# An attention and SwiGLU block on one core: the context reaches the output projection by DMA instead of by two rounds of transposes

## The chip, the cores and the metric

The kernel runs on one core of a Trainium2 chip. The metric is the device time of one execution in microseconds (us), lower is better. Before the change it was run three times: 753.49, 754.30 and 754.54 us, median 754.3 us. One more execution was profiled.

## The reference

Input `x` is (4, 1024, 128): batches, tokens, channels. With a LayerNorm `xn` of `x`, the output is `x + attention(xn) + ffn(xn)`.

```
q = xn Wq' + bq -> 16 heads of 8;  k, v = xn Wk' + bk, xn Wv' + bv -> 4 heads of 8, each shared by 4 query heads
q, k = rope(q), rope(k)
probs   = softmax(q k' / sqrt(8)) over 1024 keys
context = probs v                     # (4, 1024, 128)
attention = context Wo' + bo
ffn = (silu(xn Wg') * (xn Wu')) Wd'   # hidden 384, weights are int32 times 1/127
```

## The kernel before, in words

The attention is cut in 16 **groups**, one for each batch and key head: group `g` is batch `g // 4`, key head `g % 4`, and holds four query heads. A group runs 16 **steps**: two halves (`h`) of 512 queries by eight tiles of 128 keys. In each step:

- TensorE makes four score tiles of 128 keys x 512 queries (`scores`, line 1143) into three PSUM banks that are used in turn, and weighs the values by the probabilities of the step before (`weigh`, line 1229), all four heads into one PSUM bank, `acc_ps`, 32 rows a head: 8 rows of context, a row with the sum of the probabilities, the rest zero.
- ScalarE takes the exponential of each score tile (line 719).
- VectorE finds the row maxima for later halves from four more score tiles (`max_unit` line 1123 on TensorE, `reduce_max` line 946 on VectorE), which pass through a ring of four PSUM banks.

Beside the four maxima a step may hold a **job** that takes a slot of the same ring: the feed-forward part (`GATE`, `UP`, `DOWN`), the transposing of the negative maxima (`NEG_T`), and the context's way to the output. The table `JOB_AT` gives each step's jobs, and all engines issue in program order by it. `NEG_T` stands at steps 5 and 13: ScalarE copies its result, SyncE sends it by DMA (`load_neg`, line 434) into the rows of `qc` that the scores of the next half read two steps later.

The context's way before: when a half ends, ScalarE copies `acc_ps` to `acc_sb` (line 820). The job `CTX` at steps 8 and 16 transposes the four 128x128 tiles (line 1244) so that queries lie on partitions, and VectorE inverts the sums (line 979) and multiplies (line 981) into `ctx_all`. When the four groups of a batch are through, the job `STAGE` at step 9 transposes them back (line 1252), ScalarE copies the result to `ctx_T` (line 711; the tile is `v_T` under another name, and the profile calls it that), and `PROJ` at steps 12 and 14 multiplies by `Wo` (line 1279); VectorE adds that to `y_all` (line 998). Batch 0 is put out in groups 5 and 6, batch 1 in 9 and 10, batch 2 in 13 and 14, the first half of batch 3 in group 15. The last half of group 15 is done behind the last step (`CTX_END`, `STAGE_END`), because nothing is left to hide it.

SyncE issues the loads: at a group's start the parts for the next group's scores, after `NEG_T` of step 5 those for the maxima two groups on (`load_parts`, lines 408 to 423), each behind waits in one fixed order (`group` under `@block.sync`), and at the end the 16 stores of the output (line 506).

## Time and profile before

| | |
|---|---|
| median of three runs | 754.3 us (753.49 to 754.54) |
| profiled execution, its own time | 752.47 us |
| its span | 750.3 us |
| TensorE matmul busy | 718.9 us, 96% |
| VectorE busy | 682.7 us, 91% |
| ScalarE busy | 624.2 us, 83% |
| GpSimd busy | 227.0 us, 30% |
| DMA, mean | 51 GB/s |

The span is measured from the first to the last event of the profile; the execution's own time has 2.2 us more around it. A step is read best from the starts of `weigh` (line 1229): from one to the next is one step of all engines. A group takes 43.0 us, one that also puts out a half batch 43.4 us, and the groups fill the time from 60 us on. In these rows PE is TensorE, DVE VectorE, ACT ScalarE, POOL GpSimd, SPq the issuing of DMAs by SyncE.

### The profile page before, as it was taken

What the parts mean: (1) busy time and instruction counts of PE and PEld (TensorE: products, weight loads), DVE (VectorE), ACT (ScalarE), POOL (GpSimd) and SP (SyncE); (2) the same over time, 40 slices, a digit from 0 to 9 for tenths busy, and PEclk for the clock granted to TensorE, in tenths of its full rate; (3) what the DMA queues carried; (4) which work ended last, traced back from release to release, by engine and by line L of the source; (5) the groups of instructions that cost most, each with busy time, mean ns of one, the idle gap of its engine ahead of it and who ended that gap; (6) DMA issues with size and microseconds to landing.
All of it is one profiled execution on the core that took longest, in us unless ns stands there. A gap on an engine that the chain in (4) does not pass through costs nothing.

```text
span 750.3 us, 13756 instructions
## 1 busy us (share of the span) xinstructions
PE 718.9 (96%) x4914; PEld 216.2 (29%) x4914; DVE 682.7 (91%) x1265; ACT 624.2 (83%) x1305; POOL 227.0 (30%) x372
## 2 busy tenths in 40 slices
PE   7899999999999999999999999999999999999987
PEld 6332222222322222222322222232322222232222
DVE  6899999999999999999999999999999999999931
ACT  5638989888888988888888888889788888989886
POOL 3776552256331662112111212211121211202100
PEclk9999999999999999999999999999999999999999
DMA  9524331110311131010111101011111101110030
GB/s 298 176 65 110 117 118 33 33 34 2 117 34 33 33 115 35 5 43 19 33 33 33 33 24 43 2 34 33 33 33 33 33 2 33 33 33 2 2 85 29
DMA packets 30723, 38.26 MB, mean 51 GB/s; under 512 B 5600, under 2 KB 20448, under 8 KB 30400
## 3 DMA queue, kind: packets, MB, share of 16 engines
q1 hardware_dynamic: 27680, 30.18, 14.1%
q0 software_dynamic: 1440, 4.72, 1.7%
q10 hardware_dynamic: 1536, 2.49, 1.0%
q8 instruction: 39, 0.64, 0.4%
q14 instruction: 28, 0.23, 0.1%
HBM read 23.28 MB, written 11.53 MB: 46 GB/s over the span
## 4 chain that ended last, share of the span: by engine, by line
PE 75%; DVE 16%; ACT 6%; issue 2%; DMA 1%; SPq 0%; ACTq 0%; DVEq 0%
PE acc_ps L1229 29%; PE banks L1123 20%; DVE mx L946 13%; PE banks L1143 10%; PE banks L1096 7%; ACT probs L719 5%; PE banks L1236 4%; PE banks L1244 3%; PE banks L1063 1%; PE banks L1069 1%; DMA y_all<-in_x 1%; PE banks L1279 1%; PE banks L1252 1%; DVE stats L853 1%; DVE row_max L952 0%
## 5 line engine op out<-in xcount | busy, mean ns | idle before, releaser
L946 DVE TENSOR_REDUCE mx<-banks 128x1 f32<-128x512 f32 x1024 | 637.6, 682 | 27.1 <-PE banks L1123 24.0
L719 ACT ACTIVATE probs<-banks 128x512 f32<-128x512 f32 x1024 | 549.1, 606 | 91.3 <-PE banks L1143 86.1
L1143 PE MATMUL banks<-qc,kc 51*128 51x512 bf16 x1024 | 304.8, 382 | 10.6 <-ACT probs L719 5.5
L1123 PE MATMUL banks<-ka,qa 48*128 48x512 bf16 x1024 | 302.0, 382 | 7.1 <-DVE mx L946 6.9
L1229 PE MATMUL acc_ps<-probs,v_grp 128*32 128x512 f32 x2048 | 272.7, 605 | 1.2 <-ACT probs L719 1.0
L1123 PEld LDWEIGHTS banks<-ka,qa 48*128 48x128 bf16 x1024 | 67.2, 94 | 292.0 <-DVE mx L946 247.6
L577 POOL TENSOR_TENSOR neg_max<-row_max,nought 128x16 bf16<-128x16 f32 x32 | 7.1, 222 | 315.5 <-DVE row_max L952 310.2
L1143 PEld LDWEIGHTS banks<-qc,kc 51*128 51x128 bf16 x1024 | 64.5, 94 | 44.2 <-ACT probs L719 40.9
L1096 PE MATMUL banks<-xn_T,w_ffn 128*128 128x256 f32 x188 | 65.8, 434 | 0.0
L1229 PEld LDWEIGHTS acc_ps<-probs,v_grp 128*32 128x32 f32 x2048 | 40.3, 108 | 85.5 <-ACT probs L719 59.1
L601 POOL TENSOR_TENSOR gated<-gu 128x256 f32<-128x256 f32 x48 | 35.2, 734 | 73.7 <-ACT gu L808 73.7
L1096 PEld LDWEIGHTS banks<-xn_T,w_ffn 128*128 128x128 f32 x188 | 28.5, 189 | 38.7 <-DVE mx L946 25.1
L604 POOL TENSOR_TENSOR th<-th,gated 128x256 f32<-128x256 f32 x48 | 34.9, 726 | 3.8
L606 POOL TENSOR_TENSOR hid<-th,gated 128x256 f32<-128x256 f32 x48 | 34.9, 726 | 3.8
L1236 PE MATMUL banks<-w_ffn,hid 128*128 128x128 f32 x192 | 29.9, 292 | 0.0
L1236 PEld LDWEIGHTS banks<-w_ffn,hid 128*128 128x128 f32 x192 | 23.8, 190 | 13.7 <-DVE mx L946 6.9
L593 POOL COPY v_grp<-v_all 128x64 f32<-128x64 f32 x16 | 3.8, 239 | 70.1 <-PE acc_ps L1229 69.3
L1244 PE MATMUL banks<-ident,acc_sb 128*128 128x128 f32 x124 | 19.4, 279 | 2.8 <-ACT acc_sb L820 1.3
L820 ACT ACTIVATE acc_sb<-acc_ps 128x512 f32<-128x512 f32 x31 | 18.6, 598 | 0.5
L998 DVE TENSOR_TENSOR y_all<-y_all,banks 128x256 f32<-128x256 f32 x16 | 6.6, 412 | 12.8 <-PE banks L1279 12.8
L805 ACT ACTIVATE gu<-banks 128x256 f32<-128x256 f32 x45 | 18.1, 402 | 0.0
L1244 PEld LDWEIGHTS banks<-ident,acc_sb 128*128 128x128 f32 x124 | 13.0, 141 | 17.1 <-issue 9.3
(110 smaller groups left out, 349.3 us busy)
## 6 DMA issues: line engine op xcount, KB each, us to landing
qa<-q_rows SPq DMA_DIRECT2D x28, 192.0 KB, 3.5
qc<-q_rows SPq DMA_DIRECT2D x56, 96.0 KB, 2.6
q_rows<-part POOLq DMA_DIRECT2D x18, 256.0 KB, 4.2
ka<-k_later SPq DMA_DIRECT2D x24, 96.0 KB, 2.2
kc<-k_later SPq DMA_DIRECT2D x24, 96.0 KB, 2.2
out<-y_all SPq DMA_DIRECT2D x16, 128.0 KB, 2.0
y_all<-in_x SPq DMA_DIRECT2D x3, 512.0 KB, 12.3
k_rows<-part SPq DMA_DIRECT2D x6, 256.0 KB, 3.0
```

Of the source, the lines that this page charges most:

```text
L601: nc.gpsimd.tensor_tensor(gated[:, c, :], gu[:, c, 0:CH], gu[:, c, CH:2 * CH], ALU.mult).then_inc(gated_done, 1)
L604: nc.gpsimd.tensor_tensor(th[:, c, :], th[:, c, :], gated[:, c, :], ALU.mult).then_inc(gated_done, 1)
L606: nc.gpsimd.tensor_tensor(hid[:, c, :], th[:, c, :], gated[:, c, :], ALU.add).then_inc(hid_done, 1)
L719: nc.scalar.activation(probs[:, s % SLOTS, j, :], banks[:, score_bank(g, G * s + j), :], ACT.Exp, scale=SCALE).then_inc(exp_done, 1)
L820: nc.scalar.activation(acc_sb[:, s // NT, :], acc_ps[:, :], ACT.Copy).then_inc(acc_copied, 1)
L946: nc.vector.tensor_reduce(out=mx[:, h, col, k:k + 1], in_=ps, op=ALU.max, axis=AX.X).then_inc(max_done, 1)
L1096: nc.tensor.matmul(ps, w_ffn[:, n * HID + c * P:n * HID + (c + 1) * P], xn_T[:, chunk * CH:(chunk + 1) * CH], start=True, stop=True).then_ ...
L1123: nc.tensor.matmul(ps, qa[par][rows, j // 2, t * P:(t + 1) * P], ka[par][rows, k * W:(k + 1) * W], start=True, stop=True).then_inc(a_ready, 1)
L1143: nc.tensor.matmul(banks[:, score_bank(g, u), :], kc[par][rows, kt * P:(kt + 1) * P], qc[par][rows, h, j // 2, :], start=True, stop=True). ...
L1229: last = nc.tensor.matmul(acc_ps[VC * j:VC * (j + 1), :], v_grp[par][:, kt, :], probs[:, s % SLOTS, j, :], start=(kt == 0), stop=(kt == NT ...
L1236: last = nc.tensor.matmul(ps[:, 0:D], hid[:, c, t * P:(t + 1) * P], w_ffn[:, 2 * HID + c * D:2 * HID + (c + 1) * D], start=(c == 0), stop= ...
L1244: last = nc.tensor.transpose(ps[:, t * P:(t + 1) * P], acc_sb[:, h, t * P:(t + 1) * P], ident[:, :])
```

## The change

`CTX` and `STAGE` leave the table of jobs. SyncE moves each head's eight context rows from `acc_sb` straight to the rows of `ctx_T` that the projection reads (`move_context`): four DMAs of 8 x 512 a half. Beside each goes a DMA for the sums: for batches 0 to 2 one row of 512 to DRAM (`sums_rows`), and for batch 3 eight rows (there are eight columns of ones beside the values now) to `last_sums`. Once a batch the sums come back as 128 x 128, VectorE inverts them (`invert`), they go to DRAM again, and come back spread over eight partitions a head (`load_inverse`); VectorE multiplies `ctx_T` by them, 128 x 512 a half (`divide`). For batch 3 VectorE inverts `last_sums` itself, 128 x 512 in the last group. ScalarE's copy of `acc_ps` now waits until the half's last moves have landed. Twelve of the sixteen stores are issued ahead of the last group's moves. The end after the last step keeps its two transposes, of which the second is a matmul on the 32 rows that are new.

```diff
-JOB_AT = {..., 7: (UP, 1), 8: (CTX, 0), 10: (GATE, 2), 11: (UP, 2), 13: (NEG_T, 0), 16: (CTX, 1)}
+JOB_AT = {..., 7: (UP, 1), 10: (GATE, 2), 11: (UP, 2), 13: (NEG_T, 0)}
 def output_steps(u):
-    return {9: (STAGE, u), 12: (PROJ, 2 * u), 14: (PROJ, 2 * u + 1)}
+    return {12: (PROJ, 2 * u), 14: (PROJ, 2 * u + 1)}
 # SyncE
+            def move_context(g, h):
+                b = g // KV
+                sp.wait_ge(acc_copied, NH * g + h + 2)
+                if b > 1 and g % KV == 0:
+                    sp.wait_ge(o_ps, 2 * NH * (b - 1))
+                for j in range(G):
+                    ...
+                    sp.dma_start(ctx_T[rows, b % 2, h, :], acc_sb[VC * j:VC * j + HD, h, :]).then_inc(moved[h], 16)
+                    if b < B - 1:
+                        sp.dma_start(sums_rows[b:b + 1, n:n + W], acc_sb[VC * j + HD:VC * j + HD + 1, h, :]).then_inc(moved[h], 16)
+                    else:
+                        sp.dma_start(last_sums[rows, h, :], acc_sb[VC * j + HD:VC * j + 2 * HD, h, :]).then_inc(moved[h], 16)
             def group(g, par, left):
                 if left > 1:
                     sp.wait_ge(pv_done, STEPS * g + SLOTS)
                     load_parts(g + 1, qc[1 - par], kc[1 - par], qc_loaded[1 - par])
+                if g > 0:
+                    move_context(g - 1, 1)
                 load_neg(g, 1, par)
+                if g % KV == 0 and g > 0:
+                    load_sums(g // KV - 1)
+                if g % KV == 1 and g > KV:
+                    load_inverse(g // KV - 1)
+                if left == 1:
+                    store_out(0, 2 * OUTS - 4)
+                move_context(g, 0)
                 if g == 0:
                     ...                      # stores of the later parts, as before
                     load_parts(g + 2, qa[par], ka[par], qa_loaded[par])
+                if g % KV == 0 and g > 0:
+                    store_inverse(g // KV - 1)
                 if left > 1:
                     load_neg(g + 1, 0, 1 - par)
 # ScalarE
                         act.wait_ge(pv_done, STEPS * g + s + 1 + SLOTS)
+                        if g > 0:
+                            act.wait_ge(moved[s // NT], MOVES * g)
 # VectorE
+            def divide(u):
+                b, h = u // 2, u % 2
+                if b < B - 1:
+                    dve.wait_ge(spread_in[h], 16 * (b + 1))
+                    by = spread
+                else:
+                    dve.wait_ge(moved[h], MOVES * NG)
+                    nc.vector.reciprocal(last_sums[:, h, :], last_sums[:, h, :]).then_inc(last_inverted, 1)
+                    dve.wait_ge(last_inverted, 2)
+                    by = last_sums
+                nc.vector.tensor_tensor(ctx_T[:, b % 2, h, :], ctx_T[:, b % 2, h, :], by[:, h, :], ALU.mult).then_inc(divided, 1)
 ...
+                elif kind == GATE and n == FC - 1:
+                    if g % KV == 0 and g > 0:
+                        invert(g // KV - 1)
+                    if g in OUT_AT:
+                        divide(OUT_AT[g][12][1] // 2)
+                elif kind == NEG_T and g == NG - 1:
+                    divide_rest()
+                    divide(OUTS - 2)
 # TensorE
             def project_out(u, ps):
                 if u < 2 * OUTS - 2:
-                    pe.wait_ge(ctx_T_done, u // 2 + 1)
+                    pe.wait_ge(divided, u // 2 + 1)
```

How the instructions move, on TensorE first: around step 8 of a group, where line 1123 is a maximum's tile, 1143 a score tile, 1244 the transposes. Before:

```order
L1123 MATMUL banks<-ka,qa 128x512
L1143 MATMUL banks<-qc,kc 128x512
L1244 MATMUL banks<-ident,acc_sb 128x128 x4
L1123 MATMUL banks<-ka,qa 128x512
L1143 MATMUL banks<-qc,kc 128x512
L1229 MATMUL acc_ps<-probs,v_grp 32x512 x4
```

The same place now, the line numbers being those of the changed file:

```order
L1196 MATMUL banks<-ka,qa 128x512
L1216 MATMUL banks<-qc,kc 128x512
L1196 MATMUL banks<-ka,qa 128x512
L1216 MATMUL banks<-qc,kc 128x512
L1302 MATMUL acc_ps<-probs,v_grp 32x512 x4
```

Only the four transposes are gone between the third and the fourth pair.

SyncE's queue in the last group, before: the last negative maxima, then the stores.

```order
L434 DMA qc<-neg_max_T 3x8x128 [waits neg_T_done]
L434 DMA qc<-neg_max_T 3x8x128
L506 DMA out<-y_all 128x2x128 [waits o_done] x16
```

Now, the first of the four pairs of moves shown once:

```order
L441 DMA qc<-neg_max_T 3x8x128 [waits neg_T_done]
L441 DMA qc<-neg_max_T 3x8x128
L490 DMA out<-y_all 128x2x128 [waits o_done] x12
L502 DMA ctx_T<-acc_sb 8x512 [waits acc_copied]
L507 DMA last_sums<-acc_sb 8x512
```

Eight moves stand behind twelve stores; four stores follow them.

VectorE in the last group, behind the last row maxima, before:

```order
L952 TENSOR_TENSOR row_max<-mx 128x16 [waits max_done,neg_step]
L979 RECIPROCAL rec<-banks 128x16 [waits ctx_ps]
L981 TENSOR_TENSOR ctx_all<-banks,rec 128x4x32 [waits rec_done]
L998 TENSOR_TENSOR y_all<-y_all,banks 128x256 [waits o_ps] x2
```

Now:

```order
L1001 TENSOR_TENSOR row_max<-mx 128x16 [waits max_done,neg_step]
L1046 RECIPROCAL last_sums<-last_sums 96x512 [waits moved1]
L1048 TENSOR_TENSOR ctx_T<-ctx_T,last_sums 96x512 [waits last_inverted]
L1036 RECIPROCAL last_sums<-last_sums 128x512 [waits moved0]
L1039 TENSOR_TENSOR ctx_T<-ctx_T,last_sums 128x512 [waits last_inverted]
L1064 TENSOR_TENSOR y_all<-y_all,banks 128x256 [waits o_ps] x2
```

Two wide reciprocals and two wide products stand where a reciprocal of 16 columns and one product stood, and the second pair waits for the last group's moves.

## Rows read from the trace of the kernel before

**Rows 1.** The page: busy time of each engine, and the ending chain by engine.
```profile
PE 718.9 (96%) x4914; PEld 216.2 (29%) x4914; DVE 682.7 (91%) x1265; ACT 624.2 (83%) x1305; POOL 227.0 (30%) x372
PE 75%; DVE 16%; ACT 6%; issue 2%; DMA 1%; SPq 0%; ACTq 0%; DVEq 0%
```

**Rows 2.** Critical chain, group 7, steps 15 and 16: start us, duration us, what.
```profile
400.41 0.99 PE acc_ps L1229 x8
...
401.85 0.61 ACT probs L719
...
402.89 0.99 PE acc_ps L1229 x8
...
404.69 0.63 PE banks L1244 x4
...
405.64 0.99 PE acc_ps L1229 x8
```

**Rows 3.** Timeline of ACT there: start, us, engine, line, operation.
```profile
403.95 0.60 ACT L820 ACTIVATE acc_sb<-acc_ps 128x512 f32<-128x512 f32 x1
404.45 2.06 ACT L719 ACTIVATE probs<-banks 128x512 f32<-128x512 f32 x4
```

**Rows 4.** Critical chain, step 8 of group 7.
```profile
381.81 1.00 PE acc_ps L1229 x8
...
384.57 0.99 PE acc_ps L1229 x8
```

**Rows 5.** Critical chain, step 9 of group 6, which holds STAGE.
```profile
341.13 0.99 PE acc_ps L1229 x8
...
343.80 0.99 PE acc_ps L1229 x8
```

**Rows 6.** Timeline of DVE, group 6, first maxima of step 12.
```profile
347.85 2.48 DVE L946 TENSOR_REDUCE mx<-banks 128x1 f32<-128x512 f32 x4 [0.22 <-PE banks L1123]
```

**Rows 7.** By source line: DVE durations, ns min/median/max.
```profile
L915 DVE TENSOR_TENSOR ctx_all<-ctx_all,part x2: 689/864/1039, 16.9 to 21.0; 128x512 f32<-128x512 f32 x2
L979 DVE RECIPROCAL rec<-banks x31: 245/247/258, 83.0 to 728.5; 128x16 f32<-128x16 f32 x31
L989 DVE RECIPROCAL rec<-banks x2: 197/202/208, 744.7 to 745.1; 128x8 f32<-128x8 f32 x2
```

**Rows 8.** Timelines of ACT, SP and PE in group 0, in this order.
```profile
80.92 0.60 ACT L820 ACTIVATE acc_sb<-acc_ps 128x512 f32<-128x512 f32 x1
...
75.15 1.59 SPq L434 DMA_DIRECT2D qc<-neg_max_T  x2
...
86.60 0.90 SPq L420 DMA_DIRECT2D qa<-q_rows  x2
...
96.17 1.53 SPq L434 DMA_DIRECT2D qc<-neg_max_T  x2
...
99.38 0.60 PE L1143 MATMUL banks<-qc,kc 51*128 51x512 bf16 x2
```

**Rows 9.** Timeline of SP in group 15.
```profile
721.91 1.44 SPq L434 DMA_DIRECT2D qc<-neg_max_T  x2
723.40 6.37 SPq L506 DMA_DIRECT2D out<-y_all  x12
```

**Rows 10.** By source line: moves between places in SBUF, issue ns, then landing.
```profile
L459 SPq DMA_DIRECT2D xn<-xn x8: 586/589/686, 54.6 to 59.2; - x8
...
DMA to landing us min/median/max: 2.3/2.6/3.1
```

**Rows 11.** Timeline of PE, group 15: PROJ of step 12, and the last weigh.
```profile
736.06 0.71 PE L1279 MATMUL banks<-wf_sb,v_T 128*128 128x128 f32 x4
...
742.58 1.07 PE L1229 MATMUL acc_ps<-probs,v_grp 128*32 128x512 f32 x8 [0.57 <-ACT probs L719]
```

**Rows 12.** Windows early on: us, busy us (instructions) by engine, PEclk, DMA.
```profile
5.00:9.00 4.00, 4.00 (x21) 4.00 (x20) 2.83 (x19) 1.93 (x6) 0.00 (x0) 1.00 1.17 317
10.00:12.00 2.00, 1.87 (x17) 1.63 (x16) 2.00 (x9) 1.80 (x10) 0.00 (x0) 1.00 1.00 374
```

More of the change, by code:

```diff
@@ L78 @@
 NEG_BEHIND = HU + 5
-MAX, GATE, UP, DOWN, NEG_T, CTX, STAGE, PROJ = "max", "gate", "up", "down", "neg_T", "ctx", "stage", "proj"
+MAX, GATE, UP, DOWN, NEG_T, PROJ = "max", "gate", "up", "down", "neg_T", "proj"
 CTX_END, STAGE_END = "ctx_end", "stage_end"
-JOB_AT = {1: (DOWN, 0), 2: (DOWN, 1), 3: (GATE, 0), 4: (UP, 0), 5: (NEG_T, 1), 6: (GATE, 1), 7: (UP, 1), 8: (CTX, 0),
-          10: (GATE, 2), 11: (UP, 2), 13: (NEG_T, 0), 16: (CTX, 1)}
+JOB_AT = {1: (DOWN, 0), 2: (DOWN, 1), 3: (GATE, 0), 4: (UP, 0), 5: (NEG_T, 1), 6: (GATE, 1), 7: (UP, 1),
+          10: (GATE, 2), 11: (UP, 2), 13: (NEG_T, 0)}
 FOR_NEXT = ((GATE, 0), (UP, 0), (GATE, 1), (UP, 1), (GATE, 2), (UP, 2), (NEG_T, 0))
@@ L237, in attention_swiglu @@
         t1, t2 = (probs[:, 0, 2 * i:2 * i + 2, :].rearrange("p a c -> p (a c)") for i in range(2))
-        rot, res = (ctx_all[:, i * NT // 2:(i + 1) * NT // 2, :, :].rearrange("p t g c -> p (t g c)")[:, 0:T]
-                    for i in range(2))
+        rot, res = (tile.rearrange("p h w -> p (h w)") for tile in (ctx_T[:, 0, :, :], spread[:, :, :]))
         part = sb("part", [P, 2, PARTS, T], BF16)
@@ L385, in attention_swiglu @@
         END_T = HT // 2
+        MOVES = 16 * 2 * G
+        END_ROWS = slice(P - G * HD, P)
         @block.sync
@@ L478, in _, with store_out, load_sums, store_inverse @@
                 load_twins(b)
+            def store_out(first, last):
+                for u in range(first, last):
+                    sp.wait_ge(o_done, u + 1)
+                    sp.dma_start(out[u // 4, (u % 4) * HW:(u % 4 + 1) * HW, :].rearrange("(t p) d -> p t d", p=P),
+                                 y_all[:, u * HT // 2:(u + 1) * HT // 2, :]).then_inc(out_stored, 16)
+            def move_context(g, h):
[4 more added lines that the diff above has]
+                for j in range(G):
+                    head = g % KV * G + j
+                    rows, n = slice(head * HD, (head + 1) * HD), (h * H + head) * W
+                    sp.dma_start(ctx_T[rows, b % 2, h, :], acc_sb[VC * j:VC * j + HD, h, :]).then_inc(moved[h], 16)
+                    if b < B - 1:
+                        sp.dma_start(sums_rows[b:b + 1, n:n + W],
+                                     acc_sb[VC * j + HD:VC * j + HD + 1, h, :]).then_inc(moved[h], 16)
+                    else:
+                        sp.dma_start(last_sums[rows, h, :],
+                                     acc_sb[VC * j + HD:VC * j + 2 * HD, h, :]).then_inc(moved[h], 16)
+            def load_sums(b):
+                for h in range(NH):
+                    sp.wait_ge(moved[h], MOVES * KV * (b + 1))
+                sp.dma_start(row_sums[:, :], sums_rows[b].rearrange("(p c) -> p c", c=P)).then_inc(sums_loaded, 16)
+            def store_inverse(b):
+                sp.wait_ge(inverted, b + 1)
+                sp.dma_start(inverse_rows[b].rearrange("(p c) -> p c", c=P), row_sums[:, :]).then_inc(inverse_stored, 16)
+            def load_inverse(b):
+                sp.wait_ge(inverse_stored, 16 * (b + 1))
+                if b > 0:
+                    sp.wait_ge(divided, NH * b)
+                rows = inverse_rows[b].rearrange("(h e w) -> h e w", h=NH, e=H)
+                for h in range(NH):
+                    sp.dma_start(spread[:, h, :], rows[h].unsqueeze(1).to_broadcast([H, HD, W]))                        .then_inc(spread_in[h], 16)
             def group(g, par, left):
@@ L811, in group @@
                             copy_neg(g + 1 - n, n, bank(slot))
-                        if kind == STAGE:
-                            copy_ctx_T(n, bank(slot))
                         slot += 1
@@ L1004, in job @@
                     add_ffn(g, n, ps)
-                elif kind == CTX:
-                    normalise_context(g, n, ps)
                 elif kind == CTX_END:
@@ L1294, in bank_left @@
                     pe.wait_ge(neg_T_done, NH * g + NH * (1 - n) + n + 1)
-                elif kind == CTX:
-                    pe.wait_ge(normed, NH * g + n + 2)
                 elif kind == CTX_END:
@@ L1300, in bank_left @@
                     pe.wait_ge(end_T_done, n + 1)
-                elif kind == STAGE:
-                    pe.wait_ge(ctx_T_done, n + 1)
                 elif kind == PROJ:
@@ L1324, in take @@
                     transpose_neg(g + 1 - n, n, ps)
-                elif kind == CTX:
-                    transpose_context(g, n, ps)
                 elif kind == CTX_END:
@@ L1330, in take @@
                     stage_end(n, ps)
-                elif kind == STAGE:
-                    transpose_stage(n, ps)
                 elif kind == PROJ:
```

92 lines of the change are left out of this document (39 added, 53 removed).

## The prediction

> **What bounds the kernel.** I read the page's busy times first. TensorE is busy 96% and VectorE 91%, and the chain that ended last lies on TensorE for 75% [rows 1]. With two engines so close, the share of busy time doesn't tell what a removed instruction is worth, so I read the chain of waits through single steps, from the start of one `weigh` to the next. The reader is to see three kinds of step in it.
>
> A step without a large job takes 402.89 - 400.41 = 2.48 us [rows 2]. It isn't TensorE's own work that fills it. The chain goes from `weigh` (0.99) through the step's first score tile to ScalarE's first exponential, which starts 1.44 us after `weigh` did and takes 0.61, and back to the fourth score tile, which needs that tile's bank. It is a loop between two engines, and nothing that is taken off TensorE makes it shorter.
>
> A step with a context job takes 405.64 - 402.89 = 2.75 us at step 16 [rows 2] and 384.57 - 381.81 = 2.76 at step 8 [rows 4]. The step with `STAGE` takes 343.80 - 341.13 = 2.67 [rows 5]. So the most that a removed job can give is the distance to 2.48, not the 0.63 us that its transposes last.
>
> **What goes: the context jobs.** The copy of `acc_ps` stays, and it stands on ScalarE exactly in these steps. It starts at 403.95, right behind `weigh`, and lets the step's exponentials begin only at 404.45 [rows 3]. Without the transposes the fourth score tile is released at 404.45 + 0.61 + 0.05 = 405.11, and the next `weigh` follows 0.39 us behind, at 405.50 instead of 405.64 (0.05 and 0.39 are what lies between the same events in the step without a job: 401.85 + 0.61 to 402.89 is 0.43). So a removed `CTX` gives 0.14 to 0.15 us, not 0.27. The reciprocal of line 979 stands 31 times [rows 7], once for each job; 30 lie in groups 0 to 14, and the one in group 15 is counted with the end. 30 x 0.15 = 4.5 us. Both ends: nothing, if another wait takes the place, and 0.27 x 30 = 8.1.
>
> `STAGE` has no such copy of `acc_ps` in its step. Six of them (groups 5, 6, 9, 10, 13, 14) give 2.67 - 2.48 = 0.19 each, 1.1 us together. ScalarE's copy of it goes too, at nothing, since ScalarE waits there for scores.
>
> VectorE loses a reciprocal and a product in each context job, about half a microsecond. It is idle again by step 12 before its one tight place, where it has 0.22 us to spare [rows 6], so I count nothing for that, and the later cost of `divide` is set against it.
>
> **What comes on VectorE in the middle.** Six `divide` of 128 x 512 with both inputs in SBUF, in step 10. The nearest row took 0.69 us, and 1.04 once while GpSimd worked [rows 7]. Steps 10 and 11 last 2.7 us against some 2.45 us of maxima, so about 0.5 of it is hidden there and 0.2 in the idle time of rows 6. Three `invert` of 128 x 128: a reciprocal of 16 columns takes 247 ns and one of 8 columns 202 [rows 7], 5.6 ns a column, which makes 0.25 + 112 x 0.0056 = 0.88 us. About 0.1 us reaches the path in each of nine groups: 0.7 us with rounding up, between 0 and 2.
>
> The loads around them have room. The sums are back some 8 us before `invert`, the spread inverse some 5 us before `divide`, since both are issued behind the negative maxima of step 5.
>
> **What comes on SyncE.** Each half gets eight moves. A move between places in SBUF holds the queue for 0.59 us and the next starts 0.03 later [rows 10]: 8 x 0.62 = 5.0 us. Behind them wait the loads of the maxima's parts and then `load_neg` for the next group. From the copy of `acc_ps` to the issue of these maxima there are 96.17 - 81.5 = 14.7 us [rows 8], and the moves and four loads are issued in 7, so in a middle group it costs nothing. Group 0 differs. Its moves start at 80.92 + 0.60 = 81.5, and behind them come the later parts' stores and the loads that took SyncE from 76.7 to 87.5 [rows 8]. Now they end at 81.5 + 5.0 + 10.8 = 97.3, and the negative maxima leave at 97.3, not 96.17: 1.1 us late. They were issued by 97.70 and read at 99.38 [rows 8]. With a landing near 2 us after the second issue's start there was a margin of some 0.4, so TensorE waits 0.7 us once (0 to 1.5).
>
> **The end.** In group 15 there are no maxima after step 3, ScalarE's exponentials set the pace, and whatever blocks TensorE in its order blocks all. `PROJ` of step 12 started at 736.06 and the last `weigh` at 742.58 [rows 11]. Now this `PROJ` waits for `divided`. Step by step: the negative maxima leave SyncE until 723.35; twelve stores go until 723.40 + 6.37 = 729.77 [rows 9]; the eight moves start then, the last of them at 729.8 + 7 x 0.62 = 734.15, and it lands 2.3 us later [rows 10], at 736.4 or so. VectorE then inverts 128 x 512: 0.25 + 496 x 0.0056 = 3.0 us, by the slope of rows 7, and multiplies, 0.7. With two starts `PROJ` begins at 736.4 + 3.0 + 0.7 + 0.1 = 740.2. That is 4.1 us after it did (all in the clock of the trace before; what is gained earlier shifts everything here alike). What remains behind it is the same work as before, 6.5 us to the last `weigh`. Of the removed `CTX` and `STAGE` in this group nothing is left, since they lie ahead of the wait. The end costs 4.1 us.
>
> The reciprocal is the one operation here whose size no row shows. From below it could cost what a product of 128 x 512 does, 0.7 us, and the end would cost 1.8. From above, 247 / 16 = 15 ns for each column with no fixed part makes 7.9, and the end would cost 9.0. I take 3.0, since two widths of the same operation give the slope.
>
> The Trainium skill, "VectorE: DVE Perf Modes", section "First, the fixed hardware budget", says that the reciprocal is an iterated divide with a repeat count of 8. With the 0.96 GHz of that page's specifications, an estimate from it is 8.3 ns a column and 4.3 us for the wide one, where rows 7 show 5.6 ns. By the page the sum would be 1.3 us worse.
>
> **The sum.** -4.5 (`CTX`) - 1.1 (`STAGE`) + 0.7 (VectorE) + 0.7 (group 0) + 4.1 (end) = -0.1 us. Against the profiled execution's 752.47 that is 752.4. The median of the runs shown lies 1.8 us above that execution, so I forecast 754.2 us. A measurement of this kernel can tell about 0.2%, 1.5 us, from no change; this is within it.
>
> **Rivals.**
>
> The clock falls in the wait (the other side, slower). TensorE has nothing to do from its second score tile for step 13, near 735.3, to 740.2, almost 5 us. After the first idle 4 us of the program it made 21 records in 4 us and then 17 in 2 [rows 12], half the pace and then nearly the full one, though PEclk reads 1.00 in both rows; these are matmuls of one kind mostly. So an idle engine comes back slow, at the lower level of 1.2 GHz. If it does here, the remaining 7.5 us of matmuls (two `PROJ` at 0.64, ten scores at 0.22, four `weigh` at 0.99) take twice as long for the 4.4 us or so that it was slow at the start, so 2.2 us more, 756.4; for all of it and the small products of the end up to 9 more. Against it speaks that the idle time may be too short. It decides from the point where the wait is long enough for the clock to fall. The Trainium skill, "TensorE: Matmul & The Clock Gate", section "HAM oscillation — how this bites in real kernels", tells of a kernel that falls to half clock in every wait for a DMA; by that rule this rival would hold.
>
> The reciprocal is as fast as a product. Then the end costs 1.8, and the time is 751.9. For it: nothing in the rows but that 16 columns can't show much. Against it: the two widths.
>
> The context steps fall to 2.48 in full, since the copy on ScalarE finds another place in its queue. Then 30 x 0.12 = 3.6 us more are gained: 750.6. Rows 3 speak against it.
>
> The end's wait isn't there, because the moves are through before the projection wants them. That takes the end's 4.1 away and gives back 1.1 for the two jobs of group 15: 749.0. The stores ahead of the moves speak against it.
>
> Steady loss. The negative maxima come late in each group, or VectorE's `divide` and moves push its tight place in steps 12 to 14 on: 0.2 us in each of 15 groups makes 3.0, 757.2. For it: steps 12 to 14 are where VectorE and TensorE wait for each other already. Against it: 7 us of room on SyncE.
>
> **Chances.** Forecast 0.42 (its own range 752.4 to 755.6); clock 0.26; steady loss 0.10; fast reciprocal 0.12; steps in full 0.06; no wait at the end 0.04. Faster by over 0.2% is most of the last three: 0.20. Slower is the clock, the steady loss and the upper edge of the forecast: 0.37. Within 0.2%: 0.43. The range is 751.0 to 757.8; it takes in the clock, the steady loss and the fast reciprocal.
>
> **What would show it.** In the profile after: steps 8 and 16 at 2.61 us and step 9 of groups 5, 6 and so on at 2.48; step 16 with an exponential directly behind the copy and the fourth score tile behind that. One wait of TensorE for the negative maxima near 99 us. In the end a chain that goes stores, moves, reciprocal near 3.0 us, product, `PROJ` near 740 less what was gained before, with TensorE idle for 5 us ahead. If `weigh` takes 2 us behind it, the clock fell. I am wrong if the context steps still take 2.75, if the wide reciprocal takes under 2 us, or if groups 1 to 14 don't become shorter by 0.3 us each (0.5 with a projection).

## The result and the profile after

The changed kernel takes 760.12 us (median of five runs, 758.61 to 761.53) against 753.98 for the kernel before on the same chip (753.39 to 754.54). The ratio is 1.0086, with a 95% interval of 1.0072 to 1.0100: slower by 0.9%. The forecast was 754.2 with a range to 757.8, so the time lies outside.

The page of the kernel after has these busy times and this ending chain by engine. They answer to [rows 1].

```profile
PE 711.8 (94%) x4766; PEld 205.7 (27%) x4766; DVE 685.2 (90%) x1216; ACT 620.8 (82%) x1298; POOL 226.4 (30%) x372
PE 59%; DVE 22%; ACT 12%; issue 3%; SPq 2%; DMA 1%; ACTq 0%; DVEq 0%
```

TensorE has 148 instructions and 7.1 us of work less, in a span that is 9.0 us longer (759.3 against 750.3). Its part of the chain fell from 75% to 59%, and VectorE's rose from 16% to 22%. SyncE's queue has 2% of it, where it had nothing. So the removed work came off, and something else took more than its place.

To see where, I took the start of every `weigh` of TensorE and formed the length of each group (16 steps) from it, and beside it the head (up to the first `weigh`) and the end (group 15 and what follows). A step is counted from 1, as in the table of jobs: step 12 of a group runs from its twelfth `weigh` to its thirteenth. All in us of the profiled executions; the end is taken to the span of the page, which is rounded to 0.1:

```
                 head   grp 0  grp 2  grp 4  grp 5  grp 6  grp 12  sum of 1-14  grp 15 and end
before           60.23  43.39  43.02  43.02  43.43  43.43  43.02   604.79       41.89
after            61.38  45.88  42.75  43.05  43.18  43.18  43.40   602.31       49.73
g0_order         61.13  43.06  42.76  43.06  43.19  43.19  43.41   602.25       48.96
g0_warm24        61.64  43.06  42.76  43.06  43.19  43.19  43.41   602.26       46.74
g0_pool          61.70  43.06  42.75  42.69  43.48  42.93  42.69   600.84       48.70
one_queue        59.77  43.06  42.75  43.06  43.19  43.19  43.41   602.25       44.02
tail_fast        61.16  43.07  42.74  43.06  43.19  43.19  43.41   602.21       40.96
best             60.79  43.06  42.75  42.69  43.48  42.93  42.69   600.83       40.92
best_no_invert   61.67  43.08  42.75  42.69  42.93  42.93  42.69   599.20       40.96
```

The 9.0 us are 1.15 in the head, 2.49 in group 0, -2.48 in groups 1 to 14, and 7.84 at the end. The lower rows are experiments told below.

**A context step.** The ending chain of the kernel after, steps 15 and 16 of group 7 (start us, duration us, what), answers to [rows 2]:

```profile
402.63 0.99 PE acc_ps L1302 x8
...
404.08 0.61 ACT probs L770
...
405.12 1.04 PE acc_ps L1302 x8
406.16 0.02 issue
406.18 0.34 ACT acc_sb L871
...
406.68 0.60 ACT probs L770
...
407.71 0.97 PE acc_ps L1302 x5
```

A step without a large job still takes 405.12 - 402.63 = 2.49 us. The step with the copy takes 407.71 - 405.12 = 2.59, where it took 2.75. The chain now goes through ScalarE's copy and the exponential directly behind it, as forecast (2.61).

**VectorE in group 4.** The chain from 262 to 271 us, its pieces around `invert` (start, us, what):

```profile
261.91 0.59 DVE mx L995
262.51 0.86 DVE row_sums L1027
263.37 3.54 DVE mx L995 x6
```

By source line, durations in ns (min/median/max), for `divide` and the two wide reciprocals. They answer to [rows 7]:

```profile
L1039 DVE TENSOR_TENSOR ctx_T<-ctx_T,spread x6: 679/680/682, 305.5 to 693.3; 128x512 f32<-128x512 f32 x6
...
L1036 DVE RECIPROCAL last_sums<-last_sums x1: 3353/3353/3353, 737.9 to 737.9; 128x512 f32<-128x512 f32 x1
...
L1027 DVE RECIPROCAL row_sums<-row_sums x3: 940/940/940, 262.4 to 606.7; 128x128 f32<-128x128 f32 x3
```

The chain runs on VectorE from maximum to maximum, and the reciprocal stands in it at 0.86 of its 0.94 us. The kernel g0_pool, told below, has no `invert` in this place. Its next four maxima start after idle time, which the changed kernel no longer has:

```profile
261.28 2.48 DVE L1003 TENSOR_REDUCE mx<-banks 128x1 f32<-128x512 f32 x4 [0.22 <-PE banks L1200]
```

So a part of the reciprocal fills idle time, and the rest makes the group longer: 43.05 us against 42.69.

**Group 0.** SyncE's queue, which answers to [rows 8] (start, us, line, what):

```profile
82.69 0.70 SPq L502 DMA_DIRECT2D ctx_T<-acc_sb  x1
...
96.18 0.98 SPq L415 DMA_DIRECT2D ka<-k_rows  x2
97.20 0.90 SPq L427 DMA_DIRECT2D qa<-q_rows  x2
98.53 1.58 SPq L441 DMA_DIRECT2D qc<-neg_max_T  x2
```

And TensorE there, with the window 103 to 108 us (busy us of PE, PEld, DVE, ACT and POOL, then PEclk, share and GB/s of the DMA):

```profile
100.37 0.39 PE L1196 MATMUL banks<-ka,qa 48*128 48x512 bf16 x1
102.37 0.40 PE L1216 MATMUL banks<-qc,kc 51*128 51x512 bf16 x2 [1.61 <-issue]
...
103.81 1.60 PE L1302 MATMUL acc_ps<-probs,v_grp 128*32 128x512 f32 x8
```
```profile
103.00:108.00 5.00, 4.91 (x27) 0.98 (x25) 3.90 (x7) 4.42 (x9) 2.81 (x6) 0.66 0.87 303
```

The negative maxima left at 98.53. Less the 1.15 us that the head was later, that is 97.4, where the forecast had 97.3. But the scores that read them started at 102.37, 2.3 us after the issue of the second had ended. Before, they started 1.7 after it and did not wait. The trace's semaphore events have the landing itself. The last part of the second came 1.96 us after its issue began in the kernel before (98.94, with the scores at 99.38), and 2.90 after it now (102.28). Then the clock fell: `weigh` took 1.60 us instead of 1.06, and the granted clock was 0.66 in that window, a mean of the two levels 2.4 and 1.2 GHz.

**The end.** SyncE, then the other engines in group 15. They answer to [rows 9] and [rows 11]:

```profile
724.66 6.40 SPq L490 DMA_DIRECT2D out<-y_all  x12
731.10 0.72 SPq L502 DMA_DIRECT2D ctx_T<-acc_sb  x1
...
735.90 0.62 SPq L507 DMA_DIRECT2D last_sums<-acc_sb  x1
```
```profile
737.89 3.35 DVE L1036 RECIPROCAL last_sums<-last_sums 128x512 f32<-128x512 f32 x1 [14.28 <-DMA last_sums<-acc_sb]
741.28 0.69 DVE L1039 TENSOR_TENSOR ctx_T<-ctx_T,last_sums 128x512 f32<-128x512 f32 x1
...
742.12 1.19 PE L1336 MATMUL banks<-wf_sb,ctx_T 128*128 128x128 f32 x4 [5.87 <-DVE ctx_T L1039]
...
743.79 1.94 PE L1302 MATMUL acc_ps<-probs,v_grp 128*32 128x512 f32 x8
...
750.32 1.06 PE L1302 MATMUL acc_ps<-probs,v_grp 128*32 128x512 f32 x8 [0.68 <-ACT probs L770]
```
```profile
735.00:740.00 5.00, 1.25 (x10) 0.11 (x5) 2.10 (x1) 2.75 (x6) 0.00 (x0) 0.91 0.07 13
740.00:745.00 5.00, 2.88 (x14) 1.24 (x14) 2.36 (x3) 1.09 (x2) 0.00 (x0) 0.50 0.05 16
```

TensorE waited 5.87 us for the divided context. The first `PROJ` behind the wait took 1.19 us where it took 0.71, and the next `weigh` 1.94 instead of 1.07. The clock was 0.50 from 740 to 745, the lower level throughout. From `PROJ` to the last `weigh` it took 8.20 us, where it had taken 6.52. The last 1.3 us of the span's growth are the last store: the stores' landing, which was 1.9 us at most before, is "1.8/2.0/3.1" (min/median/max) here, and after its issue at 755.8 nothing else is left. From the start of the last `weigh` to the end of the span it takes 9.01 us here, 7.69 in the kernel before, and 7.80 to 7.82 in the profiles of all eleven experiments. So 1.2 of the 1.3 us are this execution's and not the change's.

### The profile page after: what moved, and what is told of

Its sections match the earlier page's. It is cut to its first block, busy times and chain, and to the rows that moved or that the text cites. A ratio compares the mean times of both kernels' runs of the same rounds, so it can differ in the third digit from the quotient of the medians.

```text
span 759.3 us, 13658 instructions
## 1 busy us (share of the span) xinstructions
PE 711.8 (94%) x4766; PEld 205.7 (27%) x4766; DVE 685.2 (90%) x1216; ACT 620.8 (82%) x1298; POOL 226.4 (30%) x372
## 3 DMA queue, kind: packets, MB, share of 16 engines
q10 hardware_dynamic: 1536, 2.49, 0.9%
## 4 chain that ended last, share of the span: by engine, by line
PE 59%; DVE 22%; ACT 12%; issue 3%; SPq 2%; DMA 1%; ACTq 0%; DVEq 0%
PE acc_ps L1302 25%; DVE mx L995 18%; PE banks L1196 14%; ACT probs L770 10%; PE banks L1216 9%; PE banks L1169 4%; PE banks L1309 4%; ACT acc_sb L871 1%; PE banks L1136 1%; PE banks L1336 1%; PE banks L1142 1%; SPq L490 1%; DMA y_all<-in_x 1%; DVE ctx_T L1039 1%; ACT gu L859 1%
## 5 line engine op out<-in xcount | busy, mean ns | idle before, releaser
L1196 PE MATMUL banks<-ka,qa 48*128 48x512 bf16 x1024 | 298.1, 384 | 8.9 <-DVE mx L995 8.0
L856 ACT ACTIVATE gu<-banks 128x256 f32<-128x256 f32 x45 | 18.2, 405 | 0.0
L854 ACT ACTIVATE th<-banks 128x256 f32<-128x256 f32 x45 | 17.6, 392 | 0.0
L859 ACT ACTIVATE gu<-banks 128x256 f32<-128x256 f32 x45 | 17.6, 392 | 0.0
L1336 PE MATMUL banks<-wf_sb,ctx_T 128*128 128x128 f32 x64 | 11.6, 308 | 6.0 <-DVE ctx_T L1039 5.9
```

The costliest lines, as they stand in the source:

```text
L859: nc.scalar.activation(gu[:, n, CH:2 * CH], bank(slot)[:, 0:CH], ACT.Copy).then_inc(gu_done, 1)
L1196: nc.tensor.matmul(ps, qa[par][rows, j // 2, t * P:(t + 1) * P], ka[par][rows, k * W:(k + 1) * W], start=True, stop=True).then_inc(a_ready, 1)
```

## The experiments

All ratios are against the kernel before on the same chip, whose medians there were between 753.7 and 754.0. Each edit is against the changed kernel.

**g0_order.** In group 0 alone, the moves go behind the next group's loads and its negative maxima.

```
-                move_context(g, 0)
+                if g > 0:
+                    move_context(g, 0)
...
                     load_neg(g + 1, 0, 1 - par)
+                if g == 0:
+                    move_context(0, 0)
```

> Changed kernel, but in group 0 alone SyncE issues the eight moves of the first half behind the negative maxima of group 1 instead of ahead of the later parts' stores. Theory (the loss at the change from group 0 to 1 is SyncE's order, and the slow clock behind it is a result of that wait): group 0 goes from 45.9 us back to about 43.2, its step 15 from 4.44 to 2.49, the half clock near 105 us is gone, and the time falls from 760.1 to 757.5. Rival (TensorE's clock falls there for another reason): only the 2 us of the wait go, step 16 and the next stay slow, 758.2. Rival (the maxima are ready late by themselves): no change, 760.1.

Measured: 758.17 us (757.57 to 759.97), ratio 1.0064 (1.0045 to 1.0082). Group 0 fell from 45.88 to 43.06. The queue of this kernel, and the window that had 0.66 in the changed one:

```profile
96.91 1.53 SPq L441 DMA_DIRECT2D qc<-neg_max_T  x2
98.48 0.70 SPq L502 DMA_DIRECT2D ctx_T<-acc_sb  x1
```
```profile
103.00:108.00 5.00, 4.77 (x36) 1.47 (x32) 4.89 (x10) 4.32 (x9) 2.56 (x6) 1.00 0.94 326
```

The maxima leave before the moves, the wait is gone, and the clock stays at 1.00, with 326 GB/s of DMA beside it. So the moves' place in SyncE's queue made both the wait and the fall. In the profiles it gives 2.8 us. In the medians it gives 2.0, and there the two intervals overlap (the changed kernel's is 1.0072 to 1.0100), so the size rests on the profiles.

**moves_first.** In group 15, the moves go ahead of the twelve stores of outputs: the two lines with `store_out(0, 2 * OUTS - 4)` stand behind `move_context(g, 0)`.

> Changed kernel, in the last group the eight moves of the first half are issued ahead of the twelve stores. Theory (the moves stood behind the stores): the moves start when the copy of acc_ps ends, near 729 instead of 731.1 us, so the projection starts 2.1 us earlier; idle time of TensorE 3.8 instead of 5.9 us; if the clock then doesn't fall another 1.6, so 756.4 to 758.0. Rival (the landing of the moves sets it, and the stores' traffic then collides with them): less than 1 us, 759.5.

Measured: 757.67 us (756.21 to 760.30), ratio 1.0053 (1.0033 to 1.0074). Step 12 fell from 8.93 to 6.69 us. That is 2.2 of the 6.4 that the stores take; the moves now wait for ScalarE's copy. TensorE still idles 3.64 us, and its clock still falls (0.59 from 740 to 745). The time is 2.4 us lower, near the upper end of what was expected; this interval too touches the changed kernel's.

**warm_wait.** 36 multiplies by the identity stand in TensorE's queue ahead of its wait in step 12.

```
                 if u < 2 * OUTS - 2:
+                    if u == 2 * OUTS - 4:
+                        for _ in range(36):
+                            nc.tensor.matmul(ps[:, 0:P], ident[:, :], ident[:, :], start=True, stop=True)
                     pe.wait_ge(divided, u // 2 + 1)
```

> Changed kernel with 36 matmuls of 128 x 128 on the identity put ahead of the wait of the projection in step 12 of the last group; they fill a bank that the projection overwrites. The wait itself stays. Theory (part of the end's loss is the clock that falls in the wait): granted clock 1.00 in every window of the end, the projection takes 0.64 instead of 1.19 and the weigh behind it 1.0 instead of 1.9, and the time is 1.5 to 2 us less, 758.4. Rival (behind the wait ScalarE sets the pace anyway, so the clock costs nothing): 760.1.

Measured: 760.01 us (759.21 to 762.11), ratio 1.0088 (1.0068 to 1.0109). The clock stayed at 1.00, but the 36 took 8.15 us and ended 2.4 us after the context was divided. What they saved they cost, so the run settles nothing, though its time is the rival's. It had to be repeated with fewer (g0_warm24).

**narrow_copy.** ScalarE's copy of `acc_ps` has 128 columns instead of 512 from group 1 on. The kernel leaves out the other columns of the context.

```
-nc.scalar.activation(acc_sb[:, s // NT, :], acc_ps[:, :], ACT.Copy)
+wide = W if g == 0 else P
+nc.scalar.activation(acc_sb[:, s // NT, 0:wide], acc_ps[:, 0:wide], ACT.Copy)
```

> Changed kernel, but from group 1 on ScalarE copies only the first 128 of the 512 columns of acc_ps in each half (the other columns of the context are left out; the moves stay as they are). Theory (what is left of the 2.75 us of steps 8 and 16 above 2.48 is this copy, ahead of the step's first exponential): these steps go from 2.59 to 2.48, 29 of them give 3.2 us, 756.9. Rival (another floor, such as the value matmuls waiting for the copied bank): steps stay at 2.59, 760.1.

Measured: 757.12 us (755.70 to 758.98), ratio 1.0044 (1.0026 to 1.0062). Steps 8 and 16 of groups 1 to 14 fell from 2.59 to 2.48, and group 2 from 42.75 to 42.54. The copy was the whole remainder of these steps, as the prediction had read from [rows 3].

**g0_nowide.** g0_order, with the last group's wide reciprocal on 8 columns. The kernel leaves out the inverses of the others.

```
-nc.vector.reciprocal(last_sums[:, h, :], last_sums[:, h, :])
+nc.vector.reciprocal(last_sums[:, h, 0:8], last_sums[:, h, 0:8])
```

> The changed kernel with group 0's moves behind the next loads, as in g0_order (758.17 us), and with the last group's wide reciprocal of half 0 cut from 128x512 to 128x8: the inverses of the other columns are left out. In the changed kernel's trace this reciprocal takes 3.35 us alone between the last landing and the multiply. Theory A (the chain moves, landing, reciprocal, multiply is serial and PROJ 12 waits for it): step 12 of group 15 falls from 8.9 by 3.1 us, and the time to about 755.0. Theory B (the wait also costs through TensorE's clock, and its length decides how much): step 12 falls by 3.1, and the steps behind it by another 0.5 to 1.5 us, with a granted clock of 0.8 or more in them: about 754.2. Theory C (something else, the landing or PE's own queue, ends the wait): no fall, 758.2.

Measured: 754.46 us (752.14 to 755.95), ratio 1.0007 (0.9994 to 1.0020). Step 12 fell from 8.88 to 5.56, by 3.3 us; the reciprocal now takes 0.20. The median fell by 3.7, to a time between A and B, and the chain is shown to be serial. TensorE's idle 2.67 us still end in a clock of 0.72 (735 to 740), so most of the clock's cost stayed.

**g0_warm24.** g0_order, with 24 multiplies by the identity ahead of the wait, where warm_wait had 36.

> g0_order (758.17 us) with 24 multiplies of 128x128 by the identity put into TensorE's queue ahead of its wait for the last divided context; in warm_wait 36 of them took 8.15 us (0.226 each) and ran 2.3 us past the end of the wait, so that what they saved was not seen; 24 take 5.4 of the 5.9 us of the wait. Theory A (the wait costs its own length and besides that the clock, which falls in it: PROJ 1.19 instead of 0.71 us and the steps behind it, 15.46 us for four steps in the changed kernel against 7.85 plus the wait's 5.87 at a full clock, that is 1.7 us): the granted clock stays at 1.00 from 735 on, step 12 stays near 8.5, the three behind it fall to 1.64 to 2.28, and the time to 756.7. Theory B (the steps behind are long because the queues refill, not by the clock): 758.2, with the clock at 1.00 and the steps as before.

Measured: 755.62 us (754.29 to 755.93), ratio 1.0027 (1.0015 to 1.0039). TensorE's rows around the wait, and the two windows:

```profile
733.58 5.62 PE L1334 MATMUL banks<-ident 128*128 128x128 f32 x48
...
739.41 0.71 PE L1342 MATMUL banks<-wf_sb,ctx_T 128*128 128x128 f32 x4 [0.20 <-DVE ctx_T L1042]
...
740.37 1.06 PE L1305 MATMUL acc_ps<-probs,v_grp 128*32 128x512 f32 x8
```
```profile
735.00:740.00 5.00, 4.80 (x42) 4.54 (x40) 4.04 (x2) 0.15 (x1) 0.00 (x0) 1.00 0.02 3
740.00:745.00 5.00, 5.00 (x40) 1.39 (x38) 0.84 (x2) 4.24 (x9) 0.00 (x0) 1.00 0.09 26
```

`PROJ` still waits for the same multiply, which ends as late as before: 32.39 us after group 15's first `weigh`, 32.41 in g0_order. Yet `PROJ` takes 0.71 and `weigh` 1.06, and group 15 with the end falls from 48.96 to 46.74. The medians differ by 2.5 us, or 2.2 when each is taken against the kernel before on its chip. This is the price of the clock alone, with nothing changed but what TensorE did while it waited. Theory B falls. From `PROJ` to the last `weigh` it takes 6.52 us, exactly as in the kernel before. In the changed kernel it was 8.20, so there the clock cost 1.7.

**g0_pool.** g0_order, with the six `divide` of batches 0 to 2 on GpSimd and the three `invert` in step 3 of the groups with g % 4 == 1 instead of step 10 of those with g % 4 == 0. SyncE's `store_inverse` moves along with them.

```
+                if g in OUT_AT and g < NG - 1:
+                    u = OUT_AT[g][12][1] // 2
+                    pool.wait_ge(spread_in[u % 2], 16 * (u // 2 + 1))
+                    nc.gpsimd.tensor_tensor(ctx_T[:, u // 2 % 2, u % 2, :], ctx_T[:, u // 2 % 2, u % 2, :],
+                                            spread[:, u % 2, :], ALU.mult).then_inc(divided, 1)
...
-                elif kind == GATE and n == FC - 1:
-                    if g % KV == 0 and g > 0:
-                        invert(g // KV - 1)
-                    if g in OUT_AT:
-                        divide(OUT_AT[g][12][1] // 2)
+                elif kind == GATE and n == 0 and g % KV == 1 and g > KV:
+                    invert(g // KV - 1)
```

> g0_order with the divides of batches 0 to 2 (six multiplies of 128x512) on GpSimd and the three inversions (reciprocal of 128x128) moved to step 3 of the groups with g%4==1. Theory A (VectorE's extra work delays the columns it owes ScalarE in the steps that hold it, 3.0 us over the kernel): groups 4, 5, 6, 8, 9, 10, 12, 13, 14 fall to 42.7 or, for those with the output's projection, 42.9, and the time falls by 2 to 3 us, to about 755.6. Theory B (these steps were long for another reason, the PROJ matmuls or the transfers): same as g0_order, 758.2. Theory C (GpSimd's multiply slows VectorE's own work beside it as much as it takes off it): 758.2 or slower.

Measured: 756.14 us (755.43 to 757.25), ratio 1.0030 (1.0019 to 1.0041); 2.0 less than g0_order. The profile gives 1.5 of it. Groups 4, 8 and 12 fell to 42.69, and the second group of each pair with a projection (6, 10, 14) from 43.19 to 42.93. The multiply takes longer on GpSimd, but nobody waits for it:

```profile
L705 POOL TENSOR_TENSOR ctx_T<-ctx_T,spread x6: 1278/1280/1282, 297.9 to 684.4; 128x512 f32<-128x512 f32 x6
```

Groups 5, 9 and 13, which took the reciprocal over, rose to 43.48. So it went nowhere for free: step 4, the one behind it, took 3.26 us instead of 2.70. Theory A holds for the `divide`. An `invert` costs 0.55 in the new place, where it cost 0.36 in groups 4 and 8 and 0.71 in group 12.

**tail_fast.** g0_order and moves_first; in the last group GpSimd issues half of the moves, and reciprocal and multiply go in two halves of 256 columns, the first `PROJ` waiting for the first half alone.

```
-                for j in range(G):
+                for j in range(G // 2 if (g, h) == (NG - 1, 0) else G):
...
+            pool.wait_ge(acc_copied, NH * (NG - 1) + 2)
+            for j in range(G // 2, G):
...
+                pool.dma_start(ctx_T[rows, (B - 1) % 2, 0, :], acc_sb[VC * j:VC * j + HD, 0, :]).then_inc(moved_too, 16)
+                pool.dma_start(last_sums[rows, 0, :], acc_sb[VC * j + HD:VC * j + 2 * HD, 0, :]).then_inc(moved_too, 16)
...
+                    for i in range(2):
+                        nc.vector.reciprocal(last_sums[:, h, END[i]], last_sums[:, h, END[i]]).then_inc(last_inverted, 1)
+                        dve.wait_ge(last_inverted, 2 + i)
+                        nc.vector.tensor_tensor(ctx_T[:, b % 2, h, END[i]], ctx_T[:, b % 2, h, END[i]],
+                                                last_sums[:, h, END[i]], ALU.mult).then_inc(divided, 1)
...
-                    pe.wait_ge(divided, u // 2 + 1)
+                    pe.wait_ge(divided, u // 2 + 1 + (u == 2 * OUTS - 3))
```

> g0_order, and at the end: the last group's moves ahead of the twelve stores of outputs, half of half 0's moves issued by GpSimd, and reciprocal and multiply in two halves of 256 columns, the first PROJ waiting for the first half alone. Theory A (the wait of step 12 is a serial chain of issues, landing, reciprocal and multiply): 8.9 us less 2.2 (stores), 2.0 (half reciprocal and multiply), 2 to 2.6 (four issues fewer of 0.66 each) = 2.1 to 2.7 us; time 758.2 - 6.5 = 751.7. Theory B (GpSimd's issues are slow, 1 us and more each, and its landing late): wait about 4.5, 753.7. In both the clock stays up if the wait is short; if it falls all the same, 1 us more.

Measured: 749.81 us (748.48 to 750.69), ratio 0.9947 (0.9929 to 0.9964). The first reciprocal, its multiply and `PROJ`, and the window behind them:

```profile
729.93 1.75 DVE L1048 RECIPROCAL last_sums<-last_sums 128x256 f32<-128x256 f32 x1 [9.45 <-DMA last_sums<-acc_sb]
...
731.72 0.43 DVE L1050 TENSOR_TENSOR ctx_T<-ctx_T,last_sums 128x256 f32<-128x256 f32 x1
...
733.05 0.71 PE L1350 MATMUL banks<-wf_sb,ctx_T 128*128 128x128 f32 x4
```
```profile
735.00:740.00 5.00, 4.39 (x36) 1.39 (x36) 0.42 (x1) 4.52 (x10) 0.00 (x0) 1.00 0.36 106
```

The context is divided at 732.15, and `PROJ` starts at 733.05 without a wait. Both theories had left a wait, and both were too high, A by 1.9 us. Group 15 with the end takes 40.96, 0.9 less than in the kernel before. This is the rival "no wait at the end", made true.

**one_queue.** tail_fast with all eight moves back on SyncE.

> tail_fast (749.81 us) with all eight last moves back on SyncE: half of half 0's are no longer issued by GpSimd. Moves from 725.8 on, 0.66 each to 731.1, landing 2.0 to 733.1, half a reciprocal 1.75, half a multiply 0.43: 735.3, where TensorE stood ready at 733.05. Theory A (serial chain): a wait of 2.3 us comes back in step 12 (2.28 to 4.6), the clock holding in so short a wait: 752.1. Theory B (the clock falls in a wait of 2.3 us too): 753.3. Theory C (GpSimd's share was worth nothing, the gain of tail_fast was the halving and the stores' place alone): 749.8.

Measured: 753.27 us (750.34 to 754.62), ratio 0.9993 (0.9979 to 1.0008).

```profile
733.61 0.68 PE L1342 MATMUL banks<-wf_sb,ctx_T 128*128 128x128 f32 x4 [1.84 <-DVE ctx_T L1042]
...
734.54 1.58 PE L1308 MATMUL acc_ps<-probs,v_grp 128*32 128x512 f32 x8
```
```profile
735.00:740.00 5.00, 5.00 (x32) 1.10 (x28) 1.15 (x4) 3.65 (x8) 0.00 (x0) 0.66 0.48 139
```

The four issues bring back a wait of 1.84 us, and the clock falls in it (0.66). Group 15 with the end is 3.1 us longer than in tail_fast, for 1.8 of wait. Theory B holds in this execution and by the median. The ten runs spread over 4.3 us, though, and the fastest (750.34) has a mean clock of 0.998 where the profiled one has 0.995; in it the clock can hardly have fallen at the end.

**best.** tail_fast with g0_pool's two edits.

> tail_fast and g0_pool together. If their gains add: 751.7 - 2.6 = 749.1 us, 0.6% below the kernel before. If the VectorE term is not what the trace says, 751.7. If the head's extra half-clock stretch (first weigh at 61.4 instead of 60.2 in the changed kernel) is there again, 1.1 us is lost in both sums already.

Measured: 747.87 us (747.52 to 748.49), ratio 0.9923 (0.9910 to 0.9935). It beats both kernels: 0.8% below the one before and 12.3 us below the changed one. The gains add within 0.1 us in the profile (1.4 in groups 1 to 14, nothing at the end). They are smaller than the 2.6 expected, for the reason seen in g0_pool.

**best_no_invert.** best with the three reciprocals of the row sums on 8 columns. The kernel leaves out the other inverses.

> best (747.87 us) with the three inversions of 128x128 row sums cut to 128x8, the other inverses being left out. Theory A (step 3 of groups 5, 9 and 13 is 3.26 instead of 2.70 by the 0.94 us of this reciprocal, less the idle time of 0.25 us beside it and the like): these groups fall from 43.48 to 42.95 and the time by 1.6 us, to 746.3. Theory B (the step is long for the transfers around it): same as best, 747.9.

Measured: 746.50 us (746.22 to 746.80), ratio 0.9909 (0.9895 to 0.9924). Groups 5, 9 and 13 fell to 42.93. The inversions cost 1.4 us in the medians and 1.6 in the groups. With neither operation on VectorE, groups 1 to 14 take 599.20. That is the reference by which both were priced above and below.

## Why the prediction was wrong

The signs of the sum's five terms were right, and two (`CTX` and `STAGE`) were right in size. The three costs were too small, so that a sum of -0.1 us became one of several us. Against the prediction's terms, from the profiles (us):

```
term              predicted  shown   from
CTX and STAGE     -5.6       -5.9    groups 1-14: 599.20 - 604.79, and 0.33 in group 0
VectorE           +0.7       +3.0    602.31 - 599.20, less 0.14 of late clock in group 1
group 0           +0.7       +3.0    45.88 - 43.06, and the same 0.14
the end           +4.1       +7.8    49.73 - 41.89
head              0          +1.2    61.38 - 60.23
```

**The removed jobs.** 2.59 for 2.61 us at steps 8 and 16, and 2.49 for 2.48 at step 9. narrow_copy shows that the copy sets the rest. This part was right, and right for the reason given.

**VectorE, the first step that failed.** The prediction took 0.7 us of each operation as covered: 0.5 because steps 10 and 11 last 2.7 us against 2.45 of maxima, and 0.2 of idle time from [rows 6]. Less was there. A `divide` holds the queue for 0.60 us and cost 0.26 in its group, so 0.34 were covered. An `invert` holds it for 0.86 and cost 0.36 in groups 4 and 8, so 0.50 were covered, and 0.71 in group 12. The idle time of [rows 6] lies in step 11 itself (346.43 to 349.13 by the starts of `weigh`), so the sum counted that room twice. What makes group 12 dearer is open; VectorE idles 0.46 us there ahead of `row_max`, where it idles 0.10 in group 4. The durations were right: 0.88 us was forecast for `invert` and 0.94 measured. What was wrong is how much of them was covered. The rival "steady loss" had the mechanism; it came in the steps with the new operations alone.

**Group 0.** The issue was forecast to 0.1 us, in part by luck: the moves took 4.6 us where 5.0 were forecast, and what stands behind them 11.2 instead of 10.8. The margin of 0.4 us was right for the kernel before (98.94 to 99.38). What failed is the landing, "near 2 us", which was taken over from an empty queue. In the new order the maxima go out right behind two loads of 192 KB, which take 4.0 us (median) from issue to landing and had long been through before. Windows of the kernel before, then of the kernel after:

```profile
96.00:99.00 3.00, 2.39 (x24) 0.59 (x16) 2.99 (x6) 2.70 (x7) 2.86 (x3) 1.00 0.02 4
```
```profile
97.00:99.00 2.00, 1.44 (x15) 0.34 (x7) 1.99 (x4) 1.70 (x5) 1.94 (x2) 1.00 0.76 215
```

In the four executions with the moves first in group 0 (after, moves_first, warm_wait, narrow_copy) the last part lands 2.56 to 2.90 us after the second one's issue began; in the kernel before and the eight with g0_order's edit it is 1.96 to 2.03. So the company delays the landing; whether it is the order in the queue or the traffic as such wasn't tried apart. Then the clock fell, which the prediction priced at the end only. Of the 3.0 us, 2.0 are the wait (102.37 against 100.37, g0_order's time moved by the difference of the heads) and 1.0 the clock.

**The end.** `PROJ` of step 12 starts 32.55 us after group 15's first `weigh` (742.12 - 709.57), against 27.65 (736.06 - 708.41): 4.9 us later, where 4.1 were forecast. The chain was the one written down. The reciprocal took 3.35 instead of 3.0, eight issues took 0.5 more, and the landing 0.3 less. By the estimate from the Trainium skill, "VectorE: DVE Perf Modes", section "First, the fixed hardware budget", it was to take 4.3; the measurement lies nearer to the slope of [rows 7]. What was mis-sized is what follows the wait: 1.7 us more to the last `weigh`, all by the clock, and 1.2 by the slow last landing.

**The likeliest case was the wrong one.** The rival "the clock falls in the wait" was right, and 756.4 was its time. The forecast gave it 0.26 although the idle time was known to be near 5 us. The clock cost 1.7 us in the changed kernel's profile and 2.2 to 2.5 by g0_warm24, against the 2.2 of the prediction's working. That working took the length of the slow stretch from the program's start, so the agreement is in part luck. one_queue shows that already 1.84 us of idle time can be enough. The Trainium skill, "TensorE: Matmul & The Clock Gate", section "HAM oscillation — how this bites in real kernels", tells of a kernel that falls to half clock in every wait for a DMA. This trace agrees for the wait at the end: 0.50, the lower level, all through 740 to 745.

**The head is not the change's.** Its 1.15 us go with a longer stretch at the lower level between 20 and 40 us. The windows of the kernel before, of the kernel after, and of one_queue, which does the same work there as the kernel after:

```profile
20.00:30.00 10.00, 7.22 (x35) 3.60 (x34) 9.62 (x45) 5.67 (x11) 6.61 (x14) 1.00 0.20 53
30.00:40.00 10.00, 10.00 (x37) 4.25 (x37) 8.16 (x15) 6.67 (x13) 9.69 (x18) 0.83 0.88 323
```
```profile
20.00:30.00 10.00, 7.21 (x33) 3.45 (x32) 9.69 (x44) 5.67 (x12) 6.91 (x14) 0.96 0.22 58
30.00:40.00 10.00, 10.00 (x32) 3.97 (x32) 6.68 (x12) 5.80 (x11) 9.61 (x19) 0.70 0.85 317
```
```profile
20.00:30.00 10.00, 7.21 (x33) 3.51 (x31) 9.54 (x44) 5.14 (x11) 6.78 (x14) 0.92 0.21 56
30.00:40.00 10.00, 9.95 (x40) 4.48 (x38) 8.64 (x14) 7.45 (x13) 9.61 (x19) 0.91 0.85 319
```

The changed kernels, which all do the same there, have heads from 59.77 (one_queue) to 61.70, and the kernel before has 60.23. The profiled execution of the kernel before is 1.5 us faster than its median, with a mean clock of 0.998 where 16 of the 17 runs of it beside best have 0.993 to 0.997. So the execution that was profiled was a lucky one, and the medians' difference of 6.1 us is about the 9.0 of the profiles less that, and less the late landing. For the landing speaks that the three runs of the changed kernel with the same mean clock of 0.989 took 761.46 (the profiled one), 760.12 and 760.09. What makes the head's clock vary is open.

In the medians the costs that can be taken away again are 2.0 us in group 0 (g0_order), then 8.4 at the end (tail_fast against g0_order, which includes what was gained beyond the kernel before), then 1.9 on VectorE (best against tail_fast).

## What to carry to other kernels

Where one engine works through its queue in order and near its limit, price a new wait as its length plus what the clock takes back afterwards: here 5.9 us of waiting cost another 1.7 to 2.5. Cheap ways out are another order of issues, half the work on an idle queue, or halves with the first consumer waiting for the first half alone. Before an operation is called hidden, look whether the chain runs on its engine through that place. If it does, count each idle time there once, from the rows, and don't add the difference between a step's length and the sum of its work: it is the same room.

A DMA that replaces work on an engine takes a place in a queue. Follow what stands behind it up to the first engine that waits, and count the landing in the company it then has, not as it was in an empty queue.

## What the runs showed of the hardware

- A reciprocal on VectorE takes 6.3 ns for each further column with 128 partitions (128x128 in 0.94 us, 128x256 in 1.75, 128x512 in 3.35), and a product of 128x512 from SBUF 0.68. Dividing by a reciprocal is cheap only if the reciprocal is narrow.
- The same product takes 1.28 us on GpSimd, and VectorE beside it loses nothing that can be seen: group 6 takes 42.93 us both with it and with the steps' work alone (g0_pool, best_no_invert).
- Whether a short wait lowers the clock varies. In group 0 the narrow_copy execution has the same late maxima (step 15 takes 4.22 us) and a clock of 1.00 from 103 to 108. The changed kernel has 0.66 there, and moves_first 0.50. one_queue, which waits, spreads over 4.3 us in ten runs, and best, which doesn't, over 1.0 in five. But the kernel before, which doesn't wait either, spread from 752.28 to 755.40 in fifteen, so such waits aren't the only cause of a spread.
- In group 0, loads of 6 KB landed 1.96 to 2.03 us after their issue began when nothing large stood ahead of them, and 2.56 to 2.90 right behind two loads of 192 KB.
- An issue of a move from SBUF to SBUF holds SyncE for 0.62 us though it moves 16 KB, one row to DRAM 0.41, and GpSimd issues the same move in 0.50 to 0.56.
